# Two scale instructions of VectorE take a constant tile as a second input

## The reference

```python
def fp4_quant_dequant(x):                       # BLOCK = 16, along the last dim
    xb = x.reshape(shape[:-1] + (shape[-1] // BLOCK, BLOCK))
    scale = jnp.max(jnp.abs(xb), axis=-1, keepdims=True) / 6.0
    scale = jnp.maximum(scale, jnp.float32(1e-12))
    xn = xb / scale
    idx = jnp.searchsorted(_MID, jnp.abs(xn))
    return (_GRID[idx] * jnp.sign(xn) * scale).reshape(shape)

def fp4_linear(x, w):
    return jnp.einsum('bsk,nk->bsn', fp4_quant_dequant(x), fp4_quant_dequant(w))

def _L0_ffn_ref(x, w_gate, w_up, w_down):       # 256 -> 704 -> 256
    h = silu(fp4_linear(x, w_gate)) * fp4_linear(x, w_up)
    return fp4_linear(h, w_down)

x = x + 0.5 * _L0_ffn_ref(_layernorm(x), w_gate, w_up, w_down)
x = x + _L0_attn_ref(_layernorm(x), Wq, bq, Wk, bk, Wv, bv, Wo, bo)
x = x + 0.5 * _L0_ffn_ref(_layernorm(x), w_gate, w_up, w_down)
```

## Time and profile before

| | |
|---|---|
| median of 3 runs | 1076.79 us (1076.69 to 1081.8) |
| span of the profiled execution | 1075.3 us |
| PE busy | 989.7 us (92%) |
| DVE busy | 777.9 us (72%) |
| ACT busy | 602.1 us (56%) |
| POOL busy | 379.2 us (35%) |

### The profile page before, as it was taken

How to read it: one execution, slowest core, us unless ns; L and a number is a source line. 1 busy time by engine, 2 the same in 40 slices (tenths; PEclk the granted TensorE clock), 3 DMA queues, 4 the chain that set the end, 5 groups by cost and what they waited for, 6 DMA issues and landing times.

```text
span 1075.3 us, 17149 instructions
## 1 busy us (share of the span) xinstructions
PE 989.7 (92%) x5683; PEld 853.9 (79%) x5683; DVE 777.9 (72%) x1265; ACT 602.1 (56%) x1178; POOL 379.2 (35%) x540
## 2 busy tenths in 40 slices
PE   4479999999979899999999899999997999999997
PEld 3368888888868688888888788888885888888886
DVE  7988888888848455555568455555567888888884
ACT  2557787877763444545454344545465565656654
POOL 2446767677752001000014001000003555555543
PEclk9699999999998999999999899999999999999999
DMA  9000000000000000000000000000000000000001
GB/s 320 1 0 1 1 0 0 0 0 0 1 1 2 0 1 0 0 0 0 0 1 1 1 0 0 0 0 0 0 2 0 1 20 20 20 20 0 20 20 40
DMA packets 11486, 13.17 MB, mean 12 GB/s; under 512 B 832, under 2 KB 10560, under 8 KB 11456
## 3 DMA queue, kind: packets, MB, share of 16 engines
q1 hardware_dynamic: 11456, 12.79, 3.6%
HBM read 8.59 MB, written 4.19 MB: 12 GB/s over the span
## 4 chain that ended last, share of the span: by engine, by line
PE 53%; POOL 15%; DVE 14%; issue 11%; ACT 5%; DMA 1%; POOLq 0%; SPq 0%; DVEq 0%; ACTq 0%
PE bank L1136 17%; PE bank_a L1157 11%; PE bank L1019 7%; POOL zq L382 7%; PE bank_a L1159 5%; PE bank L932 5%; POOL y L392 4%; DVE rounded L557 3%; ACT yabs L808 2%; DVE grid L563 2%; DVE probs L596 2%; PE bank L936 2%; PE bank_b L1028 2%; POOL x L399 2%; PE bank L1113 1%
## 5 line engine op out<-in xcount | busy, mean ns | idle before, releaser
L382 POOL TENSOR_TENSOR zq<-grid,s_neg 128x704 f32<-128x704 f32 (+2 forms) x192 | 143.1, 771 | 170.5 <-DVE grid L563 166.1
L1157 PE MATMUL bank_a<-v_hl,pT_hi 128*128 128x512 f32 x512 | 184.7, 403 | 0.0
L886 ACT ACTIVATE pT_hi<-bank 128x512 fp32r<-128x512 f32 x128 | 75.9, 598 | 159.2 <-PE bank L932 159.2
L323 POOL TENSOR_TENSOR var<-var,eps_all (+1 forms) x64 | 14.3, 224 | 404.7 <-ACT st_junk L774 404.7
L1019 PE MATMUL bank<-w_hi,T_hi 128*128 128x512 f32 (+1 forms) x384 | 146.7, 382 | 0.5 <-ACT T_lo L826 0.5
L1019 PE MATMUL bank<-w_hi,T_lo 128*128 128x512 f32 (+1 forms) x384 | 146.1, 380 | 0.0
L1019 PE MATMUL bank<-w_lo,T_hi 128*128 128x512 f32 (+1 forms) x384 | 146.0, 380 | 0.0
L1159 PE MATMUL bank_a<-v_hl,pT_lo 128*128 128x256 f32 x512 | 143.8, 281 | 0.0
L656 DVE TENSOR_TENSOR pT_lo<-bank,pT_hi 128x512 fp32r<-128x512 f32 x128 | 87.9, 691 | 45.6 <-ACT pT_hi L886 45.6
L797 ACT ACTIVATE silu<-bank 128x704 f32<-128x704 f32 x64 | 48.5, 758 | 128.1 <-PE bank L1019 128.1
L1136 PE MATMUL bank<-k_hi,q_hi 128*128 128x512 f32 x256 | 110.1, 430 | 7.6 <-ACT probs L881 7.6
(11 more groups left out here) (163 smaller groups left out, 2162.4 us busy)
## 6 DMA issues: line engine op xcount, KB each, us to landing
x<-in_L_attn_hidden_states SPq DMA_DIRECT2D x4, 1024.0 KB, 12.0
out<-x SPq DMA_DIRECT2D x7, 512.0 KB, 2.9
wraw<-in_L_ffn_w_down SPq DMA_DIRECT2D x1, 704.0 KB, 10.8
wraw<-in_L_ffn_w_gate SPq DMA_DIRECT2D x1, 640.0 KB, 6.7
wraw<-in_L_ffn_w_up SPq DMA_DIRECT2D x1, 640.0 KB, 7.4
wq_s<-in_L_attn_Wq SPq DMA_DIRECT2D x1, 512.0 KB, 8.1
wk_s<-in_L_attn_Wk SPq DMA_DIRECT2D x1, 512.0 KB, 8.7
wo_s<-in_L_attn_Wo SPq DMA_DIRECT2D x1, 512.0 KB, 9.4
```

The lines of the kernel that those rows point to most:

```text
L382: last = nc.gpsimd.tensor_tensor(out=blocks(zq[:, to:to + hi - lo]), in0=blocks(grid[:, lo:hi]), in1=spread(s_neg[:, par, lo // BLOCK:hi / ...
L886: nc.scalar.activation(pT_hi[:, 4 * ch:4 * ch + 4, :].rearrange("p a q -> p (a q)"), transposed(i, ch), ACT.Copy).then_inc(phi_done, 1)
L1157: nc.tensor.matmul(bank_a[:], lhsT=pT_hi[:, t, :], rhs=v_hl[:, t, :], start=t == 0, stop=False)
```

## The change

A block's two scales were made by VectorE instructions with one tensor input and two constants (`tensor_scalar`: max, then multiply). Now the second constant comes from a tile of 60 equal columns, `c_up` or `c_neg`, as a second tensor input (`scalar_tensor_tensor`). The two tiles are filled once by two memsets at the start of VectorE's stream, with a semaphore of their own. The scales of the weights in the prologue (L460, L462) stay as they are. No other instruction of any engine is added, removed or put elsewhere.

```diff
@@ -92,6 +92,8 @@
         r_all = sb("r_all", [P, NT])
+        c_up = sb("c_up", [P, ZB])
+        c_neg = sb("c_neg", [P, ZB])
@@ -193,6 +195,7 @@
         stored = sem("stored")
+        sixths = sem("sixths")
@@ -450,7 +453,10 @@
+            nc.vector.memset(c_up[:], INV_SIX_UP).then_inc(sixths, 1)
+            nc.vector.memset(c_neg[:], -1.0 / SIX).then_inc(sixths, 1)
             quarter_statistics(0)
+            dve.wait_ge(sixths, 2)
@@ -528,12 +534,12 @@
                         dve.wait_ge(amax_done, k)
-                        nc.vector.tensor_scalar(out=s_up[:, n], in0=amax[:, n], scalar1=TINY * SIX,
-                                                scalar2=INV_SIX_UP, op0=ALU.max, op1=ALU.mult).then_inc(up_done, 1)
+                        nc.vector.scalar_tensor_tensor(out=s_up[:, n], in0=amax[:, n], scalar=TINY * SIX,
+                                                       in1=c_up[:, n], op0=ALU.max, op1=ALU.mult).then_inc(up_done, 1)
                         if f or between(c, 2 - LEAD, NT - 1):
                             dve.wait_ge(zq_done, k - 2)
-                        nc.vector.tensor_scalar(out=s_neg[:, par, n], in0=amax[:, n], scalar1=TINY * SIX,
-                                                scalar2=-1.0 / SIX, op0=ALU.max, op1=ALU.mult)
+                        nc.vector.scalar_tensor_tensor(out=s_neg[:, par, n], in0=amax[:, n], scalar=TINY * SIX,
+                                                       in1=c_neg[:, n], op0=ALU.max, op1=ALU.mult)
                         dve.wait_ge(up_done, k)
```

## The result

The changed kernel is slower by a quarter of a percent: the ratio of its runs to those of the kernel before, taken beside each other, is 1.0026 with a 95% interval of [1.0017, 1.0036], which on 1077.45 us is 2.8 us (1.8 to 3.9). The medians of 14 runs each are 1081.8 us (1080.01 to 1083.0) and 1077.45 us (1076.08 to 1081.8). The profiled executions have spans of 1079.7 and 1075.3 us.

The account below looks back on a forecast made before the run. The prediction took a closed loop of GpSimd, VectorE and ScalarE as the bound, TensorE following. 54 held rounds x 0.035 us = 1.9 us made the span 1077.2; with the median 1.5 above it, 1078.7 us, range 1074.5 to 1083.

Parts of the forecast that it names:

- the hold stays: In the FFN rounds, the new s_up is held by GpSimd's running product like the old; about 0.8 us a round.
- The tail: Behind GpSimd's piece, a held new-form scale of 60 columns ends 0.09 us later, taken as 0.035 more than the old.
- Only s_neg counts: Before the reciprocal, s_neg waits for GpSimd's 64-column piece anyway, so only its 0.035 us a round gets through.
- list of things to look for: Signs in the changed profile: s_up averaging 1.0 us, s_neg about 0.36, zq pitch 7.79 to 7.82, among others.
- The sum: On the closed loop of the FFNs, 54 held rounds x 0.035 us = 1.9 us more, coming through one for one.
- left to its range: Rounds where s_neg gets ahead of GpSimd's small piece; if the longer s_up ends that, 1.2 us more.
- GpSimd loses nothing: At GpSimd's 64-column piece, the longer s_up tail of 0.09 us costs GpSimd nothing.
- free room: Between GpSimd's pieces, the first 0.10 us of a VectorE stream costs GpSimd nothing.
- A: At s_up in the FFN loop, the hold goes and TensorE becomes the bound: 1056 us; chance 0.07.
- TensorE's idle: TensorE waits for ScalarE's T_hi 0.38 us a round, 20.6 us in all; all it gives if the loop shortens.
- B: Between GpSimd's pieces, s_up isn't let in and waits for the 64-column one: +10.3 us, 1087 us; chance 0.08.
- C: In the FFN round, the added time is hidden because another link was later anyway: 1076.8 us; chance 0.10.

Follow-up runs that it names:

- e5: Changed kernel with amax in PSUM, the constant tile staying in SBUF: 1060.72 us, ratio 0.9830 to the kernel before.
- e4: Kernel before with amax in PSUM in the wide and the 44-block rounds, both scales in the old form: 1059.79 us, ratio 0.9826.
- e1: Changed kernel with s_neg back in the old form, so only s_up is new: ratio 1.0010 [0.9999, 1.0021] to the kernel before.
- e2: Changed kernel with s_up back in the old form, so only s_neg is new: ratio 1.0027 [1.0013, 1.0040] to the kernel before.
- e3: Kernel before plus only the two tiles, memsets and wait, both scales in the old form: ratio 1.0013 [1.0002, 1.0024].
- e7: Kernel before plus only tiles, memsets and wait, the same kernel as e3 on another occasion: ratio 0.9997 [0.9984, 1.0011].
- e6: Changed kernel with the two constant tiles allocated behind all others, so no other tile moves: ratio 1.0032 [1.0018, 1.0046] to the kernel before.
- e8: The changed kernel run again, beside e6 and e7: ratio 1.0027 [1.0016, 1.0038] to the kernel before.
- e9: e4 with amax in PSUM only from round 2 on, its wait for the down weights moved there: 1056.62 us, ratio 0.9804 to the kernel before.

## Why the prediction was right

**The verdict of the case, that the hold stays,** was right and came from the right rows: in the earlier trace rows instructions of the new form wait for GpSimd. e5 and e4 add what those rows couldn't show, that the same instruction is free as soon as only one input lies in SBUF.

**The tail.** Predicted 0.09 us behind GpSimd's piece by the line through 704 and 256 columns, taken as 0.035 more than now; measured 0.077 and 0.076 over the 54 rounds, for 0.049 before: 0.028 more for each, so the term was about a quarter too large. By the Trainium skill, page "VectorE: DVE Perf Modes", section "Mode 2×_2P", a one-source fp32 instruction between SBUF and SBUF reads its input through both read ports, two columns a cycle, which a two-input instruction can't, and which is not to be had with an input in PSUM. The traces agree: for the same 60 columns the tail is 0.05 us in the old form and 0.08 in the new (0.028 more, and 0.03 is half of 60 columns at the prediction's 1.03 ns), and with amax in PSUM both forms take 0.22 us.

**Only s_neg counts.** Predicted, and shown by e1 and e2 in the rows of one round and by the table. A slip in the list of things to look for: it said that s_neg would average 0.36 us. It averaged 0.323, because it starts later by what s_up became longer and its end alone is set by GpSimd; e2, where s_up kept its length, shows the 0.36.

**The sum.** 54 x 0.035 = 1.9 us predicted, 2.0 us by the table. That the two agree so well is partly luck, since the table's figure has two parts. One is the tail: in rounds in which s_neg follows GpSimd's small piece, s_inv ends 0.031 us later in the changed kernel than before, which is 54 x 0.031 = 1.7 us. The other is what the prediction had left to its range, as up to 1.2 us: in six rounds of the profile before, s_neg got ahead of GpSimd's small piece and took 0.18 us, and such a round is about 0.13 us shorter. That is also why this one pair of profiles shows 0.05 us a round and not 0.037. I counted such rounds in the other profiles: two in e3, three in e7 and two in e2, where s_up is old; none in e1, the changed kernel, e6 and e8, where s_up is new and ends later. That is 13 of 216 held rounds against none of 216. So the longer s_up does end it, and this is the one thing that s_up's form was seen to add. The measured 2.8 us (1.8 to 3.9) holds the 2.0; what lies beyond them is at least in part the clock's, by the estimate above, and the prediction had no term for it.

**GpSimd loses nothing** by the longer tail: its 64-column piece takes 0.29 us as before, as the 0.10 us of free room predicted.

**The rivals.** A (the hold goes, 1056 us) was wrong as a forecast of this change, but right as a calculation: where the hold is really taken away, the kernel comes to 1056.6 us, y comes 0.75 behind the large piece, the small one is pushed back by 0.65 to 0.94, and GpSimd's y takes 0.62, each as it was worked out. The prediction took TensorE's idle as 0.38 us a round; the 22-round stretches of e9 take 162.1 and 162.2 us for 170.7 and 171.3, 0.40 us less a round. It isn't all that one wait, though: of its 20.6 us 5.8 are left in e9, so it gave 14.8 of the 20.6 by which the time fell, and I haven't traced the rest. B (not let in between the pieces, 1087 us) never occurred: s_up follows the 704-column piece by 0.077 on the average of the 54 rounds, and its mean of 1.034 leaves no room for 1.3. C (nothing) is excluded by the interval and by the two repeats e6 and e8; one interval alone would be thin, as e3 shows. The forecast of 1078.7, worked from a median of 1076.79, meant +0.18%; measured were +0.26%, and the forecast lies at the lower end of the interval. As an absolute time 1078.7 was low: the lowest of the 14 runs took 1080.01 us, and the median of 1081.8 lies in the range of 1074.5 to 1083 thanks to the room left for scatter.

## What to carry to other kernels

When a short VectorE instruction takes several times its plain duration, look whether it ends a constant time behind a GpSimd instruction; if so, its price is GpSimd's and a cheaper form of it changes little. What frees it is where its operands lie: with one small input moved to PSUM, the one-input and the two-input form both ran beside GpSimd unhindered here. And on a closed loop of engines ask which of two neighbouring instructions is released last: a delay of the other one is swallowed.

## What the runs showed of the hardware

- A waiting VectorE instruction is let in between two GpSimd instructions that follow each other without a gap; the second of them is pushed back (0.94 us instead of 0.29, in the prologue and in e4 alike).
- Of the hold, VectorE's fixed part is hidden: behind GpSimd's end come 0.75 us for 704 columns (0.89 where nothing holds them), 0.29 for 256, 0.08 for 60 with two SBUF inputs, and 0.05 for 60 in the one-input form.
- Reading 60 columns from PSUM costs hardly more than from SBUF: 0.22 us against 0.19.
